# A macaron layer (mixture of experts, windowed attention, mixture of experts) rebuilt in three written-out phases

## What is computed

```python
x = x + 0.5 * ffn(layernorm(x))
x = x + attn(layernorm(x))
x = x + 0.5 * ffn(layernorm(x))

def ffn(x):                      # 16 experts of 64, top 4 in the best 2 of 4 groups, and one shared expert of 128
    scores = sigmoid(x @ gate_kernel)
    ...
    combine = einsum('nke,nk->ne', onehot, topk_weight)
    inter = silu(einsum('nh,ehm->enm', x, w_gate)) * einsum('nh,ehm->enm', x, w_up)
    y = einsum('ne,enh->nh', combine, einsum('enm,emh->enh', inter, w_down))
    return y + (silu(x @ sw_gate) * (x @ sw_up)) @ sw_down

def attn(x):                     # 16 query heads of 8, one key and one value head, window of 32 to both sides
    logits = einsum('btnh,bsh->bnts', q, k) / sqrt(8)
    probs = softmax(where(abs(t - s) <= 32, logits, -1e30))
    return einsum('bnts,bsh->btnh', probs, v).reshape(b, t, 128) @ Wf.T + bf
```

## Time and profile before

| | |
|---|---|
| time, median of 3 runs | 363.79 us (363.63 to 365.11) |
| profiled execution, first to last instruction (span) | 360.6 us |
| PE busy | 331.8 us, 92% |
| DVE busy | 278.0 us, 77% |
| ACT busy | 236.2 us, 66% |
| POOL busy | 172.5 us, 48% |
| DMA | 5.21 MB, nearly all in the first 18 us and in the outputs |

### The profile page before, as it was taken

One profiled execution on the slowest core, in us unless ns is written; L12 is line 12 of the kernel. 1 busy time (PEld: TensorE's weight loads), 2 busy tenths in 40 slices (PEclk: granted clock), 3 DMA queues, 4 the chain that ended last, 5 costly groups with the idle time before them and its releaser, 6 DMA issues.

```text
span 360.6 us, 6327 instructions
## 1 busy us (share of the span) xinstructions
PE 331.8 (92%) x1760; PEld 225.2 (62%) x1760; DVE 278.0 (77%) x757; ACT 236.2 (66%) x626; POOL 172.5 (48%) x171
## 2 busy tenths in 40 slices
PE   6969969789999999999999999999999989996995
PEld 2646547457676567766558766657767646764762
DVE  3885997999869858979957987957986965689552
ACT  2625735346988865888866798875888874642641
POOL 5426466734763433772523773423851425743451
PEclk9689999999999999999999999999999999999999
DMA  6600000000000000000000000000010000000101
GB/s 227 199 1 0 3 0 0 2 2 0 0 2 2 2 0 2 2 2 0 4 0 0 0 0 0 0 0 2 0 31 2 2 0 2 29 1 1 32 0 29
DMA packets 6439, 5.21 MB, mean 14 GB/s; under 512 B 1162, under 2 KB 5900, under 8 KB 6412
## 3 DMA queue, kind: packets, MB, share of 16 engines
q1 hardware_dynamic: 6412, 4.89, 4.3%
HBM read 3.84 MB, written 1.05 MB: 14 GB/s over the span
## 4 chain that ended last, share of the span: by engine, by line
PE 66%; DVE 14%; ACT 10%; issue 6%; POOL 2%; DMA 1%; DVEq 0%; ACTq 0%; POOLq 0%
PE pT L1070 7%; PE pO L1080 4%; ACT prob L492 4%; PE pY L964 4%; PE pA L1038 4%; PE pS L1113 3%; PE pS L1111 3%; PE pU L925 3%; PE pU L926 3%; PE pU L927 3%; PE pG L925 3%; PE pS L925 3%; PE pG L926 3%; PE pG L927 3%; PE pS L926 2%
## 5 line engine op out<-in xcount | busy, mean ns | idle before, releaser
L393 POOL TENSOR_TENSOR hid_hi<-hid,one 128x512 fp32r<-128x512 f32 x36 | 37.6, 1044 | 90.0 <-DVE hid L806 85.6
L492 ACT ACTIVATE prob<-pS,neg_max 128x128 f32<-128x128 f32 x256 | 73.2, 378 | 5.4 <-DVE neg_max L812 4.7
L384 POOL TENSOR_TENSOR hid<-gu,c_sb 128x512 f32<-128x512 f32 x32 | 41.0, 1285 | 40.5 <-ACT c_sb L543 21.5
L812 DVE TENSOR_REDUCE neg_max<-pS 128x4 f32<-128x512 f32 x64 | 43.8, 684 | 9.2 <-PE pS L1113 8.9
L473 ACT ACTIVATE th<-pG 128x512 f32<-128x512 f32 x54 | 32.6, 604 | 26.2 <-PE pG L927 25.2
L396 POOL TENSOR_TENSOR hid_lo<-hid,hid_hi 128x512 fp32r<-128x512 f32 x36 | 46.3, 1285 | 2.8
L782 DVE SCALAR_TENSOR_TENSOR sg<-th,pG 128x512 f32<-128x512 f32 x54 | 36.5, 676 | 14.3 <-ACT th L473 14.1
L484 ACT ACTIVATE prob_t<-pT 128x512 f32<-128x512 f32 x64 | 38.9, 607 | 11.8 <-PE pT L1070 11.8
L1070 PE MATMUL pT<-ident,prob 128*128 128x128 f32 x256 | 38.9, 274 | 5.4 <-ACT prob_t L484 5.4
L1113 PE MATMUL pS<-k_diag,q_rep 128*128 128x512 f32 x64 | 37.2, 582 | 0.0
L964 PE MATMUL pY<-hid,wd_sb 128*128 128x512 f32 x72 | 36.5, 599 | 0.6 <-POOL hid L384 0.6
(11 more groups left out here) (217 smaller groups left out, 785.5 us busy)
## 6 DMA issues: line engine op xcount, KB each, us to landing
X<-x SPq DMA_DIRECT2D x4, 256.0 KB, 7.7
out<-X SPq DMA_DIRECT2D x3, 256.0 KB, 2.3
wg_raw<-wg SPq DMA_DIRECT2D x1, 576.0 KB, 3.8
wu_raw<-wu SPq DMA_DIRECT2D x1, 576.0 KB, 4.8
wd_sb<-wd SPq DMA_DIRECT2D x1, 576.0 KB, 7.1
sel_raw<-sel_in SPq DMA_DIRECT2D x1, 512.0 KB, 6.1
out<-X SPq DMA_DIRECT2D x2, 128.0 KB, 1.9
mask_raw<-mask_in SPq DMA_DIRECT2D x1, 192.0 KB
```

The costliest lines, as they stand in the source:

```text
L384: pool.tensor_tensor(hid[:, e % HIDS, :], gu[:, e % 2, :], c_sb[:, e % 2, :], ALU.mult)\
L393: pool.tensor_tensor(hid_hi[:, e % HIDS, :], hid[:, e % HIDS, :], one[:].to_broadcast([P, SEQ]), ALU.mult).then_inc(hid_hi_done, 1)
L492: ins = act.activation(prob[:, i % 2, s, :], (pS0, pS1)[h][:, P * (s % 4):P * (s % 4 + 1)], ACT.Exp, bias=neg_max[:, s:s + 1])
L812: dve.tensor_reduce(neg_max[:, 4 * h:4 * h + 4], (pS0, pS1)[h][:].rearrange("p (s k) -> p s k", s=4), AX.X, ALU.max, negate=True).then_inc ...
```

## The change

The three stages no longer share units. The work is a list of ticks that is written out in full, with no loop in the program: ticks T = 0 to 35 are the 36 chunks of units 0 to 3, ticks 36 to 67 the 32 attention blocks of all four batches, ticks 68 to 103 the 36 chunks of units 4 to 7. The preparation of later units and batches is put at written ticks among them (`XT_AT`, `COMB_AT`, `XA_AT`, `KV_AT`, `Q_AT`, `KS_AT`, `VT_AT`).

- **SiLU table.** ACT computes SiLU from PSUM in one instruction, and DVE multiplies it by `up` in one; the tanh form took ACT one and DVE two. Exp is still used by the routing and the attention.
- **Combine weights by DMA.** The weights of a unit are transposed once (64 rows), copied, written to a DRAM buffer, and read back broadcast over 64 partitions in four DMAs of 512 KB into `c_all`. POOL multiplies all eight expert chunks of every unit with them. The `combine` matmuls, their copies and the splits of the hidden chunks go.
- **Down in rows.** `down` takes the hidden chunk as weights, four tiles of 128 tokens, and 128 columns of `wd_sb`, in float32 for all units. Tokens stand on the partitions, so the copy and the transposes of `pY` go. One matmul with zeros opens each bank.
- **Scores twice.** A first pass takes scores with queries on partitions over 96 keys per half block, for the maxima alone. The maxima are transposed on PE, copied by ACT, and multiplied by POOL into eight spare rows of the query operand. A second pass (`scores_t`) gives mask, scores and minus the maximum in one product of 128 rows, keys on partitions, so that one `exps` of 512 columns writes the probabilities where the value product needs them. The eight transposes and the copies of the probabilities go.
- **Operands of the scores.** The rows of the query operand are put together by 24 small DMAs per batch from SP, and by broadcasts of constants.
- **Others.** One query product per batch in place of four, keys and values in one, 18 routing steps in place of 23, one DVE instruction per 128 tokens for the normalisation in place of two on POOL, and 16 matmuls on zeros at the start.

```diff
+LEAD = 4
+RING = 10
+PTS = 3
...
+ATT, SECOND, END = 36, 68, 104
...
+EARLY_DOWNS = {2: (0,), 8: (1,), 9: (2, 3), 10: (4, 5), 11: (6, 7), 12: (8,), 14: (9, 10), 15: (11, 12), 16: (13, 14),
+               17: (15,), 18: (16,), 19: (17,)}
...
+            def weights(u):
+                j, run = u % 2, u // 2
+                sp.wait_ge(comb_copied, u + 1)
+                sp.dma_start(comb_dram[j].rearrange("e (r t) -> (e r) t", t=P), comb_t[:]).then_inc(comb_out[j], 16)
+                sp.wait_ge(comb_out[j], 16 * (run + 1))
+                for k in range(4):
...
+                    sp.dma_start(c_all[j][:, 2 * k:2 * k + 2, :].bitcast(F32),
+                                 comb_dram[j][:, 2 * SEQ * k:2 * SEQ * (k + 1)].unsqueeze(0)
+                                 .to_broadcast([M, 2, 2 * SEQ])).then_inc(c_in[j][k], 16)
+            def query_rows(b):
+                sp.wait_ge(q_lo_done, b + 1)
...
+                for part, src in enumerate((q_hi, q_lo, q_hi)):
+                    rows = slice(PARTS + 2 * HD * part, PARTS + 2 * HD * (part + 1))
+                    for c in range(HD):
+                        sp.dma_start(q_s[b][rows, :, c, :].bitcast(F32),
...
+            def weight(n):
...
+                pool.tensor_tensor(hid[:, n % RING, :], hid[:, n % RING, :], c_all[u % 2][:, e - 1, :].bitcast(F32), ALU.mult)\
...
+            def silu(n):
+                act.wait_ge(g_psum, n + 1)
+                if n >= 3:
+                    act.wait_ge(gu_done, n - 2)
+                act.activation(sg[:, n % 3, :], g_bank(n)[:], ACT.Silu).then_inc(silu_done, 1)
+            def exps(k, dg):
...
+                act.activation(p_t[:, k % PTS, dg, :], B[dg][:], ACT.Exp).then_inc(exp_done, 1)
+            def gate_up(n):
...
+                if n >= RING:
+                    dve.wait_ge(down_done, n - RING + 1)
+                dve.tensor_tensor(hid[:, n % RING, :], sg[:, n % 3, :], u_bank(n)[:], ALU.mult).then_inc(gu_done, 1)
+            def down(n):
...
+                    for t in tiles:
+                        ins = pe.matmul(bank[:, P * t:P * (t + 1)], hid[:, n % RING, P * t:P * (t + 1)],
+                                        wd_sb[:, e, :], start=False, stop=e == CH - 1 and t == tiles[-1])
+            for T in range(END):
+                if n is not None:
+                    gate(n)
...
+                if ATT - LEAD <= T < SECOND - LEAD:
+                    scores(T - ATT + LEAD, 0)
+                if ATT <= T < SECOND:
+                    scores_t(m, 0)
+                    if k is not None and m % 2 == 0:
+                        max_columns(k, T)
+                    if T < SECOND - LEAD:
+                        scores(m + LEAD, 1)
+                    scores_t(m, 1)
+                    if k is not None and m % 2 == 1:
+                        max_columns(k, T)
+                if n is not None:
+                    up(n)
+                if ATT <= T < SECOND + 4 and m % 2 == 0 and m >= 4:
+                    output_to_columns((m - 4) // 2, min(m + LEAD, NB * NBLK))
+                if T == 3:
+                    comb_columns(0, 0)
+                for d in downs_at(T):
+                    down(d)
+                if ATT < T <= SECOND:
+                    weighted_values(m - 1)
+                if ATT <= T <= SECOND + 1 and m % 2 == 1 and m >= 3:
+                    output_rows((m - 3) // 2)
...
+                if ATT <= T < SECOND + 4 and m % 2 == 0 and m >= 4:
+                    project((m - 4) // 2)
```

More of the change, by code:

```diff
@@ L19 @@
 F32R = mybir.dt.float32r
-BF16 = mybir.dt.bfloat16
 P = 128
@@ L581, in _, with max_copy_at @@
[L581 to L585 removed]
+                act.activation(wq_hi[:], wq_scaled[:], ACT.Copy).then_inc(attn_hi_done, 1)
+                act.activation(wkv_hi[:], wkv_raw[:], ACT.Copy).then_inc(attn_hi_done, 1)
+            def max_copy_at(T):
+                if max_block(T) is not None:
+                    max_copy(max_block(T))
@@ L1242 @@
+            down(CHUNKS - 1)
 def kernel(**inputs):
```

1822 lines of the change are left out of this document (887 added, 935 removed).

## The result

The changed kernel takes 350.55 us (median; 346.04 to 351.52) where the kernel before took 363.73 beside it: 0.958 of the time, interval 0.950 to 0.966. The forecast was 302 with a range of 282 to 328. The direction is right and the size is not: some 48 us of the expected 62 are missing. The profiled execution took 351.5, span 349.7. The ratios of this document, and the differences in brackets beside those of the medians, leave out each run that is more than 1.5% above the fastest of its kernel.

What follows compares the result with a forecast made beforehand. PE was taken to bound nearly every stage: tick 36 at 19.2 + 88.7 + 9 = 117 us, attention's end at 204, then 89 + 6.3 gives a span of 299; with 3.2 for the median, 302, range 282 to 328.

Steps and rivals of the forecast that it cites:

- ticks 36 to 67: Attention stage: PE work 69.8 us plus waits, 86 us, with half the border loads 87; tick 36 at 117, end at 204.
- a pair of attention blocks: Attention: an even tick 2.8 us with waits on ACT, an odd one 2.0, so 4.8 us a pair.
- Ticks 4 to 35 ... I take 9 us: Chunks of units 0 to 3: 88.7 us of PE work plus 9 us of stalls from DVE's bursts (2 to 20).
- hidden: Chunk phases: a pair of table loads with the Exp, 2.8 us, fits the 3.1 us a SiLU may be late.
- third rival: Table loads reach the path if a switch costs twice the load's row: 14 us more, 316; chance 0.09.
- first rival: Attention waits in series, 3.2 us a tick for 2.6, and PE may lose its clock there: about 321; chance 0.17.
- where one meets a POOL product: Ticks 4 to 35: a routing step on DVE takes 1.26 us there instead of some 0.2.
- The start: Before tick 4: routing of unit 0 2.4 us shorter, so PE goes on at 19.2 us (17.2 to 22).
- Serial attention: Attention: waits in series at 3.2 us a tick instead of 2.6 add 19 us, about 321; chance 0.17.
- ACT, DVE and PE are equally loaded: Attention: ACT 69 us, DVE 66, PE 69.8, within 5% of each other, so not all run full.
- Late weights: Fourth rival: combine weights read slowly from DRAM; gain gone at 68 GB/s, 428 us at 50 GB/s; chance 0.07.
- My sentence on `weights(3)` behind SP's issues: SP in the attention: if row DMA issues took twice as long, `weights(3)` would come four ticks late, 6 us.

Runs made afterwards that it cites:

- e18: e17 plus products of zeros on PE ahead of its waits at ticks 4, 10 and 25: 322.41 us, ratio 0.884.
- e1: Changed kernel with the reciprocal deviation of unit 1 taken on POOL before the first weight product: 341.14 us, ratio 0.936.
- e3: Changed kernel with the combine transposes of units 1 to 7 one tick later on PE and ACT: 339.53 us, ratio 0.937.
- e4: Changed kernel with a copy in place of the exponential of the router logits, so routing values differ: 340.74 us, ratio 0.930.
- e6: e5 with the gate's sigmoid taken by Tanh of half the logit instead of Exp: 327.94 us, ratio 0.899.
- e2: Changed kernel with products of zeros on PE before its waits at ticks 4, 9, 16, 25, 84 and 93: 341.96 us, ratio 0.938.
- e7: e6 plus products of zeros on PE before its waits at ticks 4, 10 and 25: 328.77 us, ratio 0.894.
- e15: e13 plus products of zeros on PE ahead of its waits at ticks 4, 10 and 25: 327.89 us, ratio 0.899.
- e14: e13 with POOL's weight product cut to 64 of 512 columns, which changes the output: 317.42 us, ratio 0.871.
- e8: e6 with POOL's weight product cut to 64 of 512 columns, which changes the output: 321.62 us, ratio 0.879.
- e10: e9 with POOL's weight product cut to 64 of 512 columns, which changes the output: 319.90 us, ratio 0.879.
- e5: Changed kernel with the edits of e1 and e3 together: 331.23 us, ratio 0.910.
- e11: e9 with the attention's input of batch 3 prepared one tick later (42 for 41): 326.53 us, ratio 0.899.
- e9: e6 with the constants of batch 1 issued on SP ahead of the weights of unit 2: 334.32 us, ratio 0.916.
- e17: e13 with batch 1's constants split on SP: q_s ones ahead of unit 2's weights, k_s ones behind batch 0's query rows: 327.12 us, ratio 0.891.
- e13: e6 with batch 3 prepared one tick later and batch 1's constants issued on SP behind the weights of unit 3: 330.23 us, ratio 0.903.

## Why the prediction was wrong

**What held.** PE decides where nothing is late, and its prices: the chunk 2.27 for 2.29, POOL's product 1.289 for 1.285, the maxima of 384 columns 0.550 for 0.55, a pair of attention blocks without other work 4.85 for 4.8. Without the late steps ticks 36 to 67 take 87.9 for 87, and tick 68 to the end 93.4 for 95.3 (e18). Fourteen table loads, as counted. The price of the pair is in part luck: the forecast had 0.8 us of waits in it, before `output_to_columns` and before `project`; PE waits some 0.4 before the first (L1116 in the waits above, 4.6 us in 12) and not at all before the second, and its own work fills 4.50 us of the pair where I had two times 1.99.

**The step that failed most: "Ticks 4 to 35 ... I take 9 us" of stalls.** There were some 29 us of waits and, by estimate, at most 13 of clock (the clock's loss times the length of the two long stretches: 0.30 x 25.6 and 0.06 x 91.5). The 131.2 us less both are 89, the 88.7 that I had as PE's work, so it is the stalls that were wrong. What each cause was worth in the whole time:

- *POOL at tick 4, 9.4 us (e1).* I let the downs be held back by the late weights, but did not ask what else stands on POOL behind the waiting product. It was the rstd of the next unit, and PE waited for it.
- *The combine transposes, 11.0 us (e3).* I counted DVE's work and its bursts, and called a late `gate_up` PE's wait. What PE waited for was the end of the routing, which the order puts one tick too early. Of the 16.4 us of this wait 9.5 lie in ticks 4 to 35, the others behind tick 68.
- *Table loads, "hidden": up to 9.8 us (e4), at most 3.3 with the transposes a tick later (e6).* I compared a pair of loads with the slack of `gate`, and not with that of what stands on DVE behind the late `gate_up`. The third rival was right that the loads reach the path, but its price was ACT's, and what counts is that of the chain behind ACT.
- *The clock, 8.6 us (e2); 1.7 to 3.3 in the later kernels (e7, e15, e18), not clear of the spread.* I had it only in the first rival, in the attention. It came behind the waits of ticks 4 to 35 as well. It shares its gain with the two orders: with fewer waits less is left.
- *DVE beside POOL, some 12 us (e14); 6.3 in e8 and 14.4 in e10, where late weights disturb the pairs.* I took 0.2 for a small step and 1.26 "where one meets a POOL product", as an exception in one group. With seven products back to back behind late weights it is the rule.

The gains overlap, so they don't make one sum; e5 shows that the first two add (19.3 of 20.4), and e6 that the loads then keep a third at most.

**The start, 24.0 for 19.3.** I took 2.4 us off the routing of unit 0 for five steps fewer. It ended at 22.8 for the 21.6 of the earlier trace rows: a step of 0.17 took 1.87 beside POOL's clearing of `k_s`, another (`r_diff`) 0.68 beside POOL's subtraction for the weights. PE's `up` of tick 3 then waits for the `gate_up` that stands on DVE behind this routing, so tick 4 begins 1.4 us after the routing's end. In e2 and e3, which leave this start as it is, the gate of tick 4 starts at 26.3 and 23.8 us, for 24.2 in the changed kernel; why it differs is open.

**The attention, 94.8 for 87.** Serial attention did not come. The excess is a normalisation ahead of the addition (2.9, e11) and a lower clock (0.96 granted in this stage, 1.00 in e18); the rest is not separated. That ACT, DVE and PE are equally loaded was wrong as well: ACT was busy 58.8 us there for the 69 that I had, DVE 68.0 for 66.

**Late weights.** I priced the read itself, and it is fast: 512 KB land in 6.4 us, and a stretch of e9 with little else in it (91 to 96 us) moves 236 GB/s, near the 227 of the earlier trace rows. In the changed kernel the price is the wait at tick 4. But once the other waits are cut, weights come late for another reason: constants fill SP's queue and the DMA engines in front of the write to DRAM (e6, e9, e17), or delay the query rows (e13). My sentence on `weights(3)` behind SP's issues had the place right and half of the reason: in e6 the weights of unit 3 were copied by 103.3, SP came to their write at 106.8, out of an issue of the masks that took 7.35 us for two, and the read could follow 4.9 us later instead of 1.8.

**What stays open.** e18 is still 20 us above the forecast, 18 in ticks 4 to 35 and 6 at the start, with some gained at the end. The short products suggest that some 12 of these are DVE beside POOL, and the wait at tick 21 is 4.5; a kernel that keeps the full product and avoids both was not tried. Of the parts of the change only the SiLU table was priced by itself; what `down` in rows, the two passes of scores and the weights by DMA give one by one is not shown.

## What to carry to other kernels

When an instruction waits for something new, list what stands behind it on its engine, in written order, and who waits for that: here a DMA wait on POOL held a normalisation, and a table load on ACT held a routing on DVE. When stages are rebuilt to fit closely, price a long wait at more than its length, since the clock behind it was lower here, and cut waits together: with one gone the next late queue, here the DMA engines full of constants, shows. Small DVE steps on SBUF should not be planned beside long POOL products.

## What the runs showed of the hardware

- From the issue of a 32 KB write to DRAM to that of the read that waits for it took 1.8 us with free DMA engines. With constants in them it took 10.2 in e17, though SP was free, and 11.6 in e9, of which SP's issue of the write took 4.0.
- SP's issue of a small row copy took 0.65 us in a quiet stretch and 1.9 beside 1.9 MB of constants (e13).
- POOL's clearings of `k_s` and `v_t` held a DVE instruction with one tensor input (`r_sum_eps`, 1.87 for the 0.17 that it takes in the kernel before; it ends at 22.24 us, and the clearing of `v_t` at 22.22), while one with two inputs beside the same clearing took its 0.22. A POOL product held both kinds (1.21 and 1.24 in e6). One instance, in the timelines of DVE and POOL in the changed kernel:

```profile
19.86 0.22 DVE L697 SCALAR_TENSOR_TENSOR r_w<-r_left,r_masked 128x64 f32<-128x64 f32 x1
...
20.37 1.87 DVE L702 TENSOR_SCALAR r_sum_eps<-r_sum 128x4 f32<-128x4 f32 x1
```

```profile
19.60 2.02 POOL L408 MEMSET k_s<- 64x2304 f32 x1
21.56 0.15 POOL L409 MEMSET neg<- 128x64 f32 x1
21.65 0.57 POOL L410 MEMSET v_t<- 8x576 f32 x1
```

- SiLU and Tanh share a table, SiLU and Exp do not (4 loads against 14).
